# Reordering the middle slot of a two-phase transformer kernel: products, gate and block statistics change places

## The reference

```
x = x + 0.5 * ffn0(layernorm(x))        # L0 ffn: int4-rounded kernel, bias, low-rank part
x = x + retention0(layernorm(x))        # 8 heads of 16, group norm, silu gate, W_O
x = x + 0.5 * ffn0(layernorm(x))
x = x + 0.5 * mod(layernorm(x))         # mixture of depths: top 256 of 512 rows
x = x + retention1(layernorm(x))        # 4 heads, keys 32, values 64, rotary, rms norm, silu gate
x = x + 0.5 * mod(layernorm(x))

mod(h): scores = h @ w_router;  the 256 rows of highest score get
        h + sigmoid(score) * (gelu(h @ W1 + b1) @ W2 + b2), the others h
```

## Time and profile before

| what | value |
|---|---|
| median of 3 runs | 814.96 us (813.86 to 816.46) |
| the profiled execution's own time | 813.06 us |
| its span, first to last instruction | 811.1 us |
| mean granted PE clock | 0.982 of full |
| busy share | PE 93%, PE weight loads 76%, DVE 82%, POOL 59%, ACT 52% |
| chain that ended last | PE 74%, DVE 17%, POOL 4%, ACT 3%, issue 2% |
| HBM traffic | 21 GB/s over the span |

### The profile page before, as it was taken

How to read it: one execution, slowest core, us unless ns; L and a number is a source line. 1 busy time by engine, 2 the same in 40 slices (tenths; PEclk the granted TensorE clock), 3 DMA queues, 4 the chain that set the end, 5 groups by cost and what they waited for, 6 DMA issues and landing times.

```text
span 811.1 us, 29578 instructions
## 1 busy us (share of the span) xinstructions
PE 756.5 (93%) x13001; PEld 612.8 (76%) x13001; DVE 666.2 (82%) x1825; ACT 424.5 (52%) x875; POOL 475.4 (59%) x375
## 2 busy tenths in 40 slices
PE   5768999999999999998789999999999999999785
PEld 4657788887888878776578888887888888888653
DVE  6687888888888999986748889987777988888777
ACT  2434555565655456564444446655544566554645
POOL 3578888888887788776333444444434344453434
PEclk9998999999999999999899999999999999999988
DMA  7000101100001000010000000000000000001113
GB/s 229 29 28 29 29 28 29 29 28 3 29 28 29 29 29 2 3 55 2 1 2 2 3 3 2 2 2 2 2 3 2 3 2 2 2 2 29 41 39 105
DMA packets 23285, 18.57 MB, mean 23 GB/s; under 512 B 2147, under 2 KB 20469, under 8 KB 22901
## 3 DMA queue, kind: packets, MB, share of 16 engines
q1 hardware_dynamic: 22596, 16.40, 6.7%
q10 hardware_dynamic: 560, 0.28, 0.1%
HBM read 12.48 MB, written 4.19 MB: 21 GB/s over the span
## 4 chain that ended last, share of the span: by engine, by line
PE 74%; DVE 17%; POOL 4%; ACT 3%; issue 2%; DMA 0%; DVEq 0%; POOLq 0%; ACTq 0%
PE ps L286 20%; PE ps L410 11%; PE ps L401 10%; PE ps L281 5%; PE ps L671 4%; PE ps L364 3%; PE ps L297 3%; PE ps L384 2%; PE ps L308 2%; PE ps L394 2%; DVE x L1221 2%; POOL grstd L1063 2%; PE ps L663 2%; PE ps L356 2%; PE ps L320 2%
## 5 line engine op out<-in xcount | busy, mean ns | idle before, releaser
L1063 POOL TENSOR_TENSOR grstd<-gve,mhalf 128x32 f32<-128x32 f32 (+1 forms) x32 | 159.0, 4968 | 26.8 <-DVE gve L1276 26.8
L410 PEld LDWEIGHTS ps<-w_s,hid 128*128 128x128 f32 x1024 | 125.4, 195 | 8.2 <-issue 7.2
L410 PE MATMUL ps<-w_s,hid 128*128 128x128 f32 x1024 | 130.3, 280 | 0.0
L401 PE MATMUL ps<-xt_r,w_s 128*128 128x512 f32 x256 | 126.6, 618 | 0.7 <-ACT xt_r L818 0.7
L822 ACT ACTIVATE hid<-ps,b_s 128x512 f32<-128x512 f32 x128 | 84.0, 725 | 25.8 <-PE ps L401 25.7
L1069 POOL TENSOR_TENSOR um<-um 128x96 f32<-128x96 f32 (+1 forms) x32 | 21.3, 665 | 90.6 <-DVE um L1255 90.6
L1059 POOL TENSOR_TENSOR r_ret<-ve_ret,powers 128x8 f32<-128x8 f32 x32 | 57.8, 1807 | 28.0 <-DVE ve_ret L1207 28.0
L401 PEld LDWEIGHTS ps<-xt_r,w_s 128*128 128x128 f32 x256 | 45.2, 191 | 36.1 <-issue 31.2
L1249 DVE TENSOR_TENSOR sc<-ps,tri 128x1024 f32<-128x1024 f32 (+1 forms) x64 | 58.3, 953 | 16.7 <-PE ps L320 10.0
L286 PE MATMUL ps<-w_qkvg,xt_p 128*128 128x128 f32 x512 | 69.4, 280 | 2.8 <-ACT xt_p L818 2.8
L1054 POOL TENSOR_TENSOR rstd_ln_mod<-ve_ln_mod,mhalf 128x4 f32<-128x4 f32 x32 | 32.3, 1010 | 65.9 <-DVE ve_ln_mod L1207 65.9
(11 more groups left out here) (236 smaller groups left out, 1748.5 us busy)
## 6 DMA issues: line engine op xcount, KB each, us to landing
xtin<-in_xt SPq DMA_DIRECT2D x16, 256.0 KB, 3.6
out_x<-base SPq DMA_DIRECT2D x16, 256.0 KB, 2.3
xin<-in_x SPq DMA_DIRECT2D x15, 256.0 KB, 3.0
rot<-in_rot SPq DMA_DIRECT2D x2, 1024.0 KB, 5.9
w_s<-in_w SPq DMA_DIRECT2D x2, 256.0 KB
xin<-in_x ACTq DMA_DIRECT2D x1, 256.0 KB, 4.0
w_qkvg<-in_wqkvg SPq DMA_DIRECT2D x1, 256.0 KB, 3.8
w_qkv<-in_wqkv SPq DMA_DIRECT2D x1, 256.0 KB
```

What stands on the lines that cost most here:

```text
L401: nc.tensor.matmul(bank(k), w1_s[:, f, :], xt["r"][:].rearrange("p j n -> p (j n)"), start=True, stop=True).then_inc(s[f"h{f}"], 1)
L410: mm = nc.tensor.matmul(bank(k, j * P, P), hid[:, f, j * P:(j + 1) * P], w2_s[:, f, :], start=False, stop=(f == last and j == NT - 1), ski ...
L1063: nc.gpsimd.tensor_tensor(grstd[:, 0:n], gve[:, 0:n], mhalf[:, 0:n], ALU.pow) \
```

## The change

In `slot_a`, which affects the last slot of phase A only (number 15, the one that prepares no batch), `routed_up(3)` goes ahead of the wait for `xt["c"]` and of `ffn2`. In the middle slot on PE: the last of the four down products goes behind the transposes of `x1`; `routed_up(2)` goes ahead of the output product; the down products of batch 14 are split, two ahead of the state products and two behind them, into bank 0 (read by `store_y`) in place of bank 2, and no longer wait for `qm`. In the first slot of phase B the wait for `ystore` moves from the start to just ahead of the value products, which write bank 0. On DVE in the middle slot `block_sum(1)` and `block_statistics(1)` go ahead of `x2`, and `gate_b` ahead of `x3`.

```diff
@@ slot_a, PE
                 if sl.prepare:
                     tilewise(tiles(AT["g"]), xt["p"], w_qkvg[:, 3, :], "g_mm")
+                if route and not sl.prepare:
+                    routed_up(3, up[3])
                 if sl.complete:
                     wait(pe, "ln_f2_xt", old)
                     tilewise(tiles(AT["ffn2"]), xt["c"], w_ffn[:], "ffn2")
                 if route:
                     if sl.prepare:
                         wait(pe, "v", new)
-                    routed_up(3, up[3])
+                        routed_up(3, up[3])
                     routed_up(2, up[2])
@@ slot_ab, PE
-                for f in range(NF):
+                for f in range(NF - 1):
                     routed_down(f, X1, last)
                 wait(pe, "x1", new)
                 pe.wait_ge(s["w_step"], W_STEPS)
                 transpose4("ln_ret", x1[sb.buf(1, 4)], 0)
+                routed_down(NF - 1, X1, last)
                 wait(pe, "ln_ret_xt", new)
...
+                wait(pe, "act0", done)
+                routed_up(2, YB)
                 wait(pe, "gt", old)
                 tilewise(tiles(CB), gt[:, 0, :].rearrange("p (j n) -> p j n", j=NT), w_o0[:], "wo")
-                wait(pe, "act0", done)
-                routed_up(2, YB)
...
                 wait(pe, "v", new)
+                routed_down(0, 0, done)
+                routed_down(1, 0, done)
                 wait(pe, "gate", new)
                 states_b(range(NT), True, X1, sb)
-                wait(pe, "qm", new)
-                for f in range(NF):
-                    routed_down(f, 2, done)
+                routed_down(2, 0, done)
+                routed_down(3, 0, done)
@@ slot_b, PE
-                if not sl.complete:
-                    wait(pe, "ystore", sl.count(-2))
                 rank_bank(g - 1)
...
                 if sl.complete:
                     wait(pe, "x2", old)
+                if not sl.complete:
+                    wait(pe, "ystore", sl.count(-2))
                 tilewise(tiles(BT["v"], VF), xt["p"], w_qkv1[:, 2 * P:], "v_mm")
@@ slot_ab, ACT
-                store_y(2, sa.batch(-2), done)
+                store_y(0, sa.batch(-2), done)
@@ slot_ab, DVE
                 keep_base(sa.batch(-2), done)
+                block_sum(1)
+                block_statistics(1)
                 wait(dve, "base", done)
                 scaled_sum(CB, r_ret[sa.buf(-1, 4)][:, 0, :], x1[sa.buf(-1, 4)], x2, "wo", "x2", old)
                 variance("ln_f2", x2, ve["ln_f2"], old)
                 rotate(new)
                 router_sum(sa.batch(-2), done)
+                gate_b(X1, sb)
                 wait(dve, "x2b", old)
                 wait(dve, "ln_f2_rstd", old)
                 scaled_sum(CB, rstd["ln_f2"], x2b, x2, "ffn2", "x3", old)
                 variance("ln_mod", x2, ve["ln_mod"], old)
-                gate_b(X1, sb)
                 keep_states_b(X1, new)
-                block_sum(1)
-                block_statistics(1)
```

## The result

The changed kernel takes 805.12 us (median of 4 runs, 803.58 to 807.99), the kernel before 815.52 (4 runs, 813.86 to 816.46): a ratio of 0.988, 95% interval 0.986 to 0.9901. Timed again beside the last experiments it took 805.74 (5 runs, 801.62 to 806.84) against 815.3, ratio 0.9868 [0.9848, 0.9888]. The forecast was 805.6 in a range of 803.6 to 808.6, made from a median of 814.96 for the kernel before.

What follows compares the result with a forecast made beforehand. PE bounds the kernel, so only its waits around the middle slot can be won: waits 7.3 us plus slow clock 2.5, less a new wait of 0.4, give 9.4; 814.96 - 9.4 = 805.6 us, range 803.6 to 808.6.

Steps and rivals of the forecast that it cites:

- middle stretch: From the start of slot 15's `ffn2` to slot 17's first scores: 9.45 us less, scores at 399.9 instead of 409.35.
- Slot 15: `routed_up(3)` fills the 1.30 us wait ahead of `ffn2`, so the down products start 0.87 us sooner.
- Fourth down product: Start of middle slot: its 0.89 us covers PE's 0.67 us wait for the copied x1.
- `routed_up(2)` with the gelu's wait: Middle slot: it fills the 0.81 us wait ahead of `wo`; the 0.43 us wait for the gelu goes too.
- Store wait: Start of slot 17: moving PE's wait for the routed output's store takes out 0.68 us, hidden behind scores, masks and attention.
- Gate and split: Middle slot: PE's 3.85 us wait for DVE's gate goes, and the slow clock's 2.5 us with it.
- The new wait: Middle slot, behind `wo` and an up product: PE waits 0.4 us for x2, the only new wait found.
- The margins: Spare before PE needs each: gate 1.2 us, `um` for slot 17's scores 0.35, POOL's state sums for the carry products 0.9.
- Clock 1.00 throughout: Sign of being right: PE's granted clock stays at 1.00 from slot 15's last products to slot 17's first scores.
- Rival (a): The clock falls anyway in the thinner middle slot: the 2.5 us stays, 808.1 us; chance 8%.
- rival (b): DVE becomes the bound as margins ahead of x2 (0.1) and `um` (0.35) fail: 806.6 to 808.1 us; chance 12%.
- Rivals (c) and (d): (c) PE waits in slot 17 instead, 812.5 us, 4%; (d) a new wait repeats in phase B's slots, 818.4, 2%.

Runs made afterwards that it cites:

- the last experiments: Three alterations of the changed kernel: slot 17's order 805.73 us, POOL's router product moved behind `x2b` 805.26, both together 804.15; kernel before beside them 815.3.
- a second profile: The changed kernel, unaltered, profiled again: middle stretch 26.56 us as in the first profile; 805.74 us (5 runs).
- the gate alone: The kernel before with only DVE's `gate_b` moved ahead of x3: 809.93 us (10 runs), ratio 0.9941.
- router product late: The changed kernel with POOL's `router_product` behind `x2b` and its sum at the end of DVE's slot: 805.26 us (4 runs).
- up product 3: The changed kernel with `routed_up(3)` put back behind `ffn2` in slot 15: 805.77 us (1 run).
- down product 4: The changed kernel with the fourth down product of batch 13 put back ahead of the transposes of x1: 804.4 us (1 run).

## Why the prediction was right

**The size.** Predicted for the middle stretch was 9.45 less, measured 9.43, and the same in a second profile. The median was predicted at 805.6 and measured at 805.12 and 805.74. That both agree so closely is partly luck. Single executions ran from 801.62 to 807.99, and against the kernel before the two measurements give 10.4 and 9.6 less. And inside the stretch two errors cancel: PE reached the states 23.79 behind `ffn2` (401.61 - 377.82) where the working had 23.9, and took 2.77 from there to the scores (404.38 - 401.61) where it had 2.6.

**Term by term.** Slot 15: 0.87 predicted, 0.65 lost when undone. Fourth down product: 0.67 predicted, 0.68 lost. `routed_up(2)` with the gelu's wait: 0.81 + 0.43 predicted, 0.68 lost when undone. Store wait: 0.68 predicted, 0.75 lost. Gate and split: 3.85 and the clock's 2.5; the gate alone gave 2.61 + 2.46 = 5.07 and the split another 1.2. Undone, two of the four short terms cost less than the waits that came back, since PE's wait for x2 shrank or went at the same time. So the terms are not free of each other.

**The new wait** was predicted at 0.4 and is 0.63 (0.44 in five of the variants). Two terms make it. PE came sooner: queries and keys held it for 1.83 (385.72 to 387.55), and I had charged 2.05. And x2 came hardly sooner than forecast, 16.5 behind `ffn2` for 16.6, although the work ahead did, by 0.3 (`wo` 15.06 behind `ffn2` for 15.3). The step at fault is DVE's part ahead of x2: I looked for POOL's disturbance at the block sum, which took 1.13 as when undisturbed, and missed that the earlier gy would fall beside POOL's router product. That product stood still, 11.55 behind `ffn2` in both kernels, while gy went from 14.02 to 12.27. It took 1.10 where it took 0.68 before:

```profile
387.38 0.68 DVE L1578 TENSOR_TENSOR t<-t,gate 128x512 f32<-128x512 f32 x1
```

and, in the changed kernel, beside the gy of 390.09 shown above:

```profile
389.37 1.27 POOL L1087 TENSOR_TENSOR rp<-h,wr_b 128x512 f32<-128x512 f32 x1
```

With the router product late it takes 0.68 again, and x2 starts 16.34 behind `ffn2` (389.02 - 372.68), 0.18 sooner. It also takes 0.68 with up product 3 or down product 4 put back, where gy comes later and behind the router product; that is why x2's wait is 0.44 there. The Trainium skill (SBUF — State Buffer, Who interferes with whom) says that a DVE instruction with two SBUF inputs contends with a GpSimd one that reads SBUF; the trace agrees, with gy at 1.10 beside the router product and 0.68 without it.

**The margins** held: ahead of the gate 1.2 was predicted and 0.84 measured (the gate came 0.16 later and PE 0.15 sooner than in the working), ahead of the scores' wait for `um` 0.35 and 0.33, and behind the state sums 0.9 and 0.76 (they end at 406.58, the carry products start at 407.34).

**Not as said.** "Clock 1.00 throughout" was right for the middle slot and not for slot 17 in the first profile. Rival (a) had the clock fall in the thin middle slot, where it never did without a wait of over two microseconds for the gate. A loss of its kind came behind the mask wait, that I left standing as free of charge. My argument against (a), that the clock held 1.00 with PE busy for 7.04 of 10, was weak: earlier in the same profile of the kernel before it was 0.66 with PE busy for 7.15 of 10:

```profile
60.00:70.00 10.00, 7.15 (x150) 5.80 (x151) 7.12 (x26) 3.64 (x8) 9.69 (x9) 0.66 0.16 47
```

So the busy share alone doesn't tell whether the clock holds. Of rival (b) a little came: the margin of 0.1 ahead of x2 did fail, since DVE sets x2's start, but it cost 0.2 and not 0.5, and nothing behind it was late. Rivals (c) and (d) didn't come: slot 17's scores have no wait, its wait for the mask is 1.47 to the hundredth, and what lies behind its value products took 392.4 and 393.8 in the two profiles for 394.33 before, so no new wait repeats in phase B.

## What to carry to other kernels

Where one engine is full almost everywhere, list its waits by place and sum the work between them; a reordering is worth about the waits that it fills, and one long wait can cost its length and a slow clock behind it. When an instruction moves earlier, look at what runs on the other engine at its new time, not only at the instruction that was moved on purpose. Where the runs of one program scatter by several microseconds, measure a part of 0.7 us between two fixed instructions in the trace.

## What the runs showed of the hardware

PE's clock fell behind a wait of 3.85 and of 2.61 in the middle slot, and never behind those of 1.24 (two kernels) or less there. Behind the mask wait of 1.47 it fell in five profiles of eleven, the same program once with and once without. The fall costs 1.6 us there. Only small products (scores and four transposes) stand just ahead of that wait; whether that plays a part, no run shows. DVE's gy, reading two SBUF tensors, took 1.10 beside a POOL product of 1.27 that began 0.7 us ahead of it, and 0.68 without; POOL's root of ln_f2 took 1.93 in this slot, before and in every profile that has its record, and about 1.0 elsewhere, always beside DVE's rotate, which reads two SBUF tensors too; no run separated them.
